# Perceiver block on one core: second values read the stored norm, last residual moved to VectorE, order of the last two batches and of the mean changed

## The reference

```
x = x + xattn(layernorm(x), ctx, mask) @ W_o + b_o   # 8 heads of 64, keys from ctx (8, 2048, 384)
h = layernorm(x)                                     # "the second norm"
x = x + attn(h @ Wq, h @ Wkv) @ Wo                   # 16 heads, attends over the 8 batches' axis
x = x + bitlinear_ffn(layernorm(x))                  # weights rounded to -1, 0, 1 times mean(|w|)
```

## Time and profile before

| what | value |
|---|---|
| runs | 795.01 us median of 3 (793.55 to 796.64) |
| the profiled execution's own time | 799.53 us |
| its span | 797.6 us |
| PE busy | 674.9 us, 85% of the span |
| DVE / ACT / POOL busy | 442.4 / 372.3 / 109.7 us |
| mean granted TensorE clock | 0.931 |

### The profile page before, as it was taken

One profiled execution on the slowest core, in us unless ns is written; L12 is line 12 of the kernel. 1 busy time (PEld: TensorE's weight loads), 2 busy tenths in 40 slices (PEclk: granted clock), 3 DMA queues, 4 the chain that ended last, 5 costly groups with the idle time before them and its releaser, 6 DMA issues.

```text
span 797.6 us, 15089 instructions
## 1 busy us (share of the span) xinstructions
PE 674.9 (85%) x4274; PEld 526.5 (66%) x4274; DVE 442.4 (55%) x972; ACT 372.3 (47%) x872; POOL 109.7 (14%) x152
## 2 busy tenths in 40 slices
PE   3988597969889688969949979999999899889994
PEld 2767486858778577858738757777777778535542
DVE  5742343544535453444547746666666445698860
ACT  3234243424334333434424336666665343478883
POOL 2481000010100110010120002222222100012211
PEclk9998797979989797989969989999999899999998
DMA  8010000000000000003238934444443333001011
GB/s 299 5 44 21 4 19 20 21 21 21 2 20 21 21 2 20 21 21 113 86 119 317 322 112 159 159 159 159 159 159 138 140 122 117 1 1 27 13 27 39
DMA packets 40081, 64.84 MB, mean 81 GB/s; under 512 B 4074, under 2 KB 20458, under 8 KB 40050
## 3 DMA queue, kind: packets, MB, share of 16 engines
q1 hardware_dynamic: 40050, 64.45, 24.2%
HBM read 53.95 MB, written 10.49 MB: 81 GB/s over the span
## 4 chain that ended last, share of the span: by engine, by line
PE 70%; issue 11%; DVE 10%; ACT 3%; DVEq 3%; POOL 1%; DMA 1%; ACTq 0%; SPq 0%; POOLq 0%
PE bank L571 41%; PE bank L706 6%; PE bank L923 5%; PE bank L694 3%; PE bank L931 3%; PE bank L679 2%; PE bank L841 2%; DVE tern L1630 2%; PE bank L818 1%; PE bank L873 1%; DMA wq_raw<-in_L_xattn_W_q_dram 1%; PE bank L829 1%; DVE wqk_odd_lo L1327 1%; ACT cxT_hi L999 1%; DVE h_f L1735 1%
## 5 line engine op out<-in xcount | busy, mean ns | idle before, releaser
L1016 ACT ACTIVATE probs<-probs,negm 128x256 f32<-128x256 f32 x104 | 52.2, 503 | 105.5 <-DVE negm L1452 105.5
L1452 DVE CUSTOM_DVE_ANT_0 probs<-bank,bias,negm_old 128x256 f32<-128x256 f32 x104 | 46.0, 480 | 60.3 <-PE bank L679 58.1
L679 PE MATMUL bank<-kT_hi,qT_hi 64*128 64x256 f32 x104 | 23.2, 443 | 48.6 <-issue 44.5
L923 PE MATMUL bank<-w_T,xqT 128*128 128x512 bf16 x256 | 58.4, 379 | 4.6 <-ACT xqT L1212 2.0
L468 POOL TENSOR_TENSOR rstd<-var_eps,neg_half 128x1 f32 (+1 forms) x16 | 10.4, 652 | 337.8 <-DVE var_eps L1515 265.8
L706 PEld LDWEIGHTS bank<-v_sb,pT 128*128 128x128 f32 x416 | 52.4, 191 | 5.5
L706 PE MATMUL bank<-v_sb,pT 128*128 128x64 f32 x416 | 54.7, 274 | 0.0
L1327 DVE TENSOR_TENSOR kT_lo<-bank,kT_hi 128x512 fp32r<-128x512 f32 x28 | 19.4, 692 | 61.2 <-ACT kT_hi L1005 61.2
L1009 ACT COPY v_sb<-bank 128x512 f32<-128x512 f32 x28 | 15.1, 590 | 76.5 <-PE bank L706 73.5
L679 PEld LDWEIGHTS bank<-kT_hi,qT_hi 64*128 64x128 f32 x104 | 11.4, 214 | 58.3 <-issue 46.7
L923 PEld LDWEIGHTS bank<-w_T,xqT 128*128 128x128 bf16 x256 | 24.1, 98 | 34.8 <-issue 2.9
(11 more groups left out here) (226 smaller groups left out, 1717.1 us busy)
## 6 DMA issues: line engine op xcount, KB each, us to landing
tern_dram<-tern SPq DMA_DIRECT2D x8, 768.0 KB, 5.4
tstage<-tern_dram SPq DMA_DIRECT2D x8, 768.0 KB, 4.7
cx<-in_ctx_dram SPq DMA_DIRECT2D x14, 384.0 KB, 2.9
absw<-in_L_ffn_w_gate_dram SPq DMA_DIRECT2D x8, 512.0 KB, 3.8
absw<-in_L_ffn_w_up_dram SPq DMA_DIRECT2D x8, 512.0 KB, 5.2
absw<-in_L_ffn_w_down_dram SPq DMA_DIRECT2D x8, 512.0 KB, 6.1
tern_raw<-in_L_ffn_w_gate_dram SPq DMA_DIRECT2D x8, 512.0 KB, 6.2
tern_raw<-in_L_ffn_w_up_dram SPq DMA_DIRECT2D x8, 512.0 KB, 7.0
```

The costliest lines, as they stand in the source:

```text
L679: last = mm(bank[3 + j][:, 0:CHUNK], part(qT, a)[o:o + DH, g, :], part(kT, c)[o:o + DH, g, :], start=(a == c), stop=(a == "lo"))
L923: last = mm(bank[3 + 2 * which + c % 2][:], xqT[:, u, k * P:(k + 1) * P], w_T[:, which, k, c * 512:c * 512 + 512], start=(k == 0), stop=(k ...
L1016: fn(probs[:, h, :], probs[:, h, :], ACT.Exp, bias=negm[:, h:h + 1], scale=-1.0, accum_out=csum[:, h:h + 1]).then_inc(p_done, 1)
L1452: nc.vector.tensor_tensor_reduce(probs[:, h, :], bank[3 + h % 2][:, 0:CHUNK], bias[:], -SCALE, negm_old[:, h:h + 1], ALU.add, ALU.min, neg ...
```

## The change

1. The second values read `ln_T` itself instead of the copy `lnT_g`. The copies are gone from ACT, and the loop over groups on PE becomes straight code. The first product waits for each part that it needs and no longer for all of `wv2_lo`.
2. The residual of batch 7 is added by DVE straight from bank 4 (`residual_last`). ACT's copy to `xo` and POOL's addition of that batch are gone.
3. The norms of batches 6 and 7 use two slots of `stats` and `mv` and are interleaved; `values_low` is placed between them in another order.
4. SP issues the first piece of |w| once the last projection has ended, then the store of batch 7, the second piece, and, after all stores have landed, the first query/key weights. Before, all of these waited for the last `norm_low`.
5. DVE runs `weights_low(0)` ahead of the sums of |w| instead of behind them.
6. PE does the mean and the wait for DVE's last value copy between `project(0, 0)` and `project(0, 1)`, instead of ahead of both.

```diff
 # SP
-            with sp.Fori(0, B) as b:
+            def keep_x(b):
                 sp.wait_ge(x_mid, START + b + 1)
-                sp.dma_start(x_mid_dram[bass.ds(b, 1)].rearrange("a p d -> p (a d)"), tile_of(x_all, b)).then_inc(x_mid_out, 16)
-
-            sp.wait_ge(lnT_lo, START + B)
-            sp.wait_ge(x_mid_out, 16 * B)
-            for g in range(G):
-                if g >= 2:
-                    sp.wait_ge(absw_done, START + g - 1)
+                sp.dma_start(x_mid_dram[b], x_all[:, b, :]).then_inc(x_mid_out, 16)
+
+            def load_abs(g):
                 to = absw[g % 2]
...
+            for b in range(B - 1):
+                keep_x(b)
+            sp.wait_ge(xo_ps, START + B)
+            load_abs(0)
+            keep_x(B - 1)
+            load_abs(1)
+            sp.wait_ge(x_mid_out, 16 * B)
+            sp.dma_start(wqk_raw[:, 0:DK, :], wq2_v[:, :, 0:P]).then_inc(wqk_in, 16)
+            sp.dma_start(wqk_raw[:, DK:2 * DK, :], wkv_v[:, :, 0:P]).then_inc(wqk_in, 16)
+            for g in range(2, G):
+                sp.wait_ge(absw_done, START + g - 1)
+                load_abs(g)
 # POOL
-            with pool.Fori(1, B) as b:
+            with pool.Fori(1, B - 1) as b:
                 rsqrt(b - 1, var_c, rstd_c)
                 residual(b)
+            rsqrt(B - 2, var_c, rstd_c)
             rsqrt(B - 1, var_c, rstd_c)
 # PE
-            pe.wait_ge(wv2_lo, START + DK)
-            with pe.Fori(0, G // 2) as t:
...
+            def second_values(g, half):
+                def waits(a, b, k):
+                    if g == 0 and half == 0:
+                        if a == "lo" and k == 0:
+                            pe.wait_ge(lnT_lo, START + B)
+                        elif b == "lo":
+                            pe.wait_ge(wv2_lo, START + k + 1)
+                        elif a == "hi":
+                            pe.wait_ge(wv2_hi, START + k + 1)
+
+                product(bank[2 * (g % 2) + half][:], lambda k, w: part(ln_T, w)[:, k, g * P:(g + 1) * P],
+                        lambda k, w: part(wv2, w)[:, k, half * 512:half * 512 + 512], DK, waits).then_inc(v2_ps, 1)
+
+            pe.wait_ge(lnT_hi, START + B)
+            for g in range(G):
+                if g >= 2:
+                    pe.wait_ge(v2_act, START + g - 1)
+                    pe.wait_ge(v2_dve, START + g - 1)
+                second_values(g, 0)
+                second_values(g, 1)
...
             for u in range(UNITS):
                 project(u, 0)
+                if u == 0:
+                    mean_weights()
+                    pe.wait_ge(v2_dve, START + G)
                 project(u, 1)
 # ACT
             for k in range(DK):
-                if k == DK - 1:
-                    projected(B - 1)
                 cp(wv2.hi[:, k, :], wv2_raw[:, k, :]).then_inc(wv2_hi, 1)
...
-            group_copy(0, 0)
-            group_copy(1, 1)
             weights_high(0)
             with act.Fori(0, G // 2) as t:
...
-                    group_copy(g + 2, u)
 # DVE
+            def residual_last():
+                dve.wait_ge(xo_ps, START + B)
+                dve.wait_ge(x_mid, START + B - 1)
+                tt(x_all[:, B - 1, :], x_all[:, B - 1, :], bank[4][:], ALU.add).then_inc(x_mid, 1)
+
+            norm_stats(B - 2)
             values_low(0)
-            norm_stats(B - 2)
+            residual_last()
+            norm_stats(B - 1, 1)
+            norm(B - 2)
             values_low(1)
-            norm(B - 2)
+            norm(B - 1, 1)
             norm_low(B - 2)
-            norm_stats(B - 1)
             values_low(2)
-            norm(B - 1)
+            norm_low(B - 1)
             values_low(3)
-            norm_low(B - 1)
...
+            weights_low(0)
             with dve.Fori(0, G // 2) as t:
...
-            weights_low(0)
```

More of the change, by code:

```diff
@@ L153, in bass_perceiver_block_kernel @@
         wv2 = Split("wv2", 88, DK, HD2)
-        lnT_g = Split("lnT_g", 48, 2, D)
         absw = [at("absw0", 56, 3, PIECE), at("absw1", 68, 3, PIECE)]
@@ L216, in bass_perceiver_block_kernel @@
         (wq_hi, wk_hi, wo_hi, xnT_hi, q_done, qT_hi, cxT_hi, kT_hi, v_done, p_done, alpha_done, pT_act, onT_hi, lnT_hi, xo_done,
-         wv2_hi, lnTg_done, v2_act, wqk_hi, qT2_done, p2_done, pT2_act, tern_rounded, wo2_hi, oT_hi, wT_act,
+         wv2_hi, v2_act, wqk_hi, qT2_done, p2_done, pT2_act, tern_rounded, wo2_hi, oT_hi, wT_act,
          xq_done, xqT_done, sg_done, h_round, hq_done, hqT_done, y_scaled) = sems(
             "act", "wq_hi wk_hi wo_hi xnT_hi q_done qT_hi cxT_hi kT_hi v_done p_done alpha_done pT_act onT_hi lnT_hi xo_done "
-            "wv2_hi lnTg_done v2_act wqk_hi qT2_done p2_done pT2_act tern_rounded wo2_hi oT_hi wT_act "
+            "wv2_hi v2_act wqk_hi qT2_done p2_done pT2_act tern_rounded wo2_hi oT_hi wT_act "
             "xq_done xqT_done sg_done h_round hq_done hqT_done y_scaled")
@@ L366, in _ @@
                 sp.dma_start(to[:, 2, :].rearrange("p (t i) -> p t i", t=DK), down_v[g]).then_inc(absw_in[g % 2], 16)
-                if g == 0:
-                    sp.dma_start(wqk_raw[:, 0:DK, :], wq2_v[:, :, 0:P]).then_inc(wqk_in, 16)
-                    sp.dma_start(wqk_raw[:, DK:2 * DK, :], wkv_v[:, :, 0:P]).then_inc(wqk_in, 16)
+            for b in range(B - 1):
[10 more added lines that the diff above has]
+                load_abs(g)
             def load_weights(piece, slot):
@@ L778, in _, with mean_weights @@
             turn_norm(B - 1)
-            pe.wait_ge(wv2_lo, START + DK)
-            with pe.Fori(0, G // 2) as t:
[L782 to L791, removed]
+            def second_values(g, half):
[16 more added lines that the diff above has]
+                second_values(g, 1)
+            def mean_weights():
+                pe.wait_ge(asum_done, START + 1)
+                mm(bank[4][:, 0:3], ones[:], asum3[:], start=True, stop=True).then_inc(mean_ps, 1)
             pe.wait_ge(v2_act, START + G)
-            pe.wait_ge(v2_dve, START + G)
             def project(u, which):
@@ L1094, in _ @@
             norm_high(B - 1)
[L1095 to L1103, removed]
             def weights_high(m):
@@ L1507, in norm_low, with norm_stats, norm @@
                 low(of(ln_T.lo), bank[6][:].rearrange("p (k g q) -> p k g q", k=DK, q=16), of(ln_T.hi)).then_inc(lnT_lo, 1)
-            def norm_stats(b):
+            def norm_stats(b, slot=0):
                 dve.wait_ge(x_mid, START + b + 1)
                 settle()
-                own(dve, ln_step_c, 2 * b, nc.vector.bn_stats(stats[:, 0, :], tile_of(x_all, b)), 1)
+                own(dve, ln_step_c, 2 * b, nc.vector.bn_stats(stats[:, slot, :], tile_of(x_all, b)), 1)
                 settle()
-                own(dve, ln_step_c, 2 * b, nc.vector.bn_aggr(mv[:, 0, :], stats[:, 0, :]), 2)
-                ts(var_eps[:, bass.ds(within(b), 1)], mv[:, 0, 1:2], EPS, None, ALU.add).then_inc(var_c, 1)
-            def norm(b):
+                own(dve, ln_step_c, 2 * b, nc.vector.bn_aggr(mv[:, slot, :], stats[:, slot, :]), 2)
+                ts(var_eps[:, bass.ds(within(b), 1)], mv[:, slot, 1:2], EPS, None, ALU.add).then_inc(var_c, 1)
+            def norm(b, slot=0):
                 dve.wait_ge(rstd_c, START + b + 1)
                 dve.wait_ge(lnT_ps, START + b)
-                ts(xn_c[:], tile_of(x_all, b), mv[:, 0, 0:1], rstd[:, bass.ds(within(b), 1)], ALU.subtract, ALU.mult).then_inc(xn_c_done, 1)
+                ts(xn_c[:], tile_of(x_all, b), mv[:, slot, 0:1], rstd[:, bass.ds(within(b), 1)], ALU.subtract, ALU.mult).then_inc(xn_c_done, 1)
             def query_low(b):
@@ L1557, in values_low, with weights_low @@
                 low(wv2.lo[:, k, :], wv2_raw[:, k, :], wv2.hi[:, k, :]).then_inc(wv2_lo, 1)
+            def residual_last():
[3 more added lines that the diff above has]
+            norm_stats(B - 2)
             values_low(0)
-            norm_stats(B - 2)
+            residual_last()
+            norm_stats(B - 1, 1)
+            norm(B - 2)
             values_low(1)
-            norm(B - 2)
+            norm(B - 1, 1)
             norm_low(B - 2)
-            norm_stats(B - 1)
             values_low(2)
-            norm(B - 1)
+            norm_low(B - 1)
             values_low(3)
-            norm_low(B - 1)
+            def weights_low(m):
+                dve.wait_ge(wqk_hi, START + m + 1)
+                low(wqk_lo_of[m % 2][:], wqk_raw[:], wqk_hi_of[m % 2][:]).then_inc(wqk_lo, 1)
+            weights_low(0)
             with dve.Fori(0, G // 2) as t:
@@ L1578, in _ @@
                     tc(v_all[:, bass.ds(g, 1), 512:1024].rearrange("p a n -> p (a n)"), bank[2 * u + 1][:]).then_inc(v2_dve, 1)
-            def weights_low(m):
-                dve.wait_ge(wqk_hi, START + m + 1)
-                low(wqk_lo_of[m % 2][:], wqk_raw[:], wqk_hi_of[m % 2][:]).then_inc(wqk_lo, 1)
-            weights_low(0)
             dve.wait_ge(absw_done, START + G)
```

## The result

The changed kernel is faster. In the comparison that the forecast was made for, it takes 787.9 us (median of 4, 785.57 to 790.62) against 795.83 before (median of 4); the ratio, estimated from all runs of the comparison, is 0.9894, 95% interval 0.9863 to 0.9925, that is 8.4 us (6.0 to 10.9), and the two medians differ by 7.9. Two later comparisons of the same kernels gave 0.9863 (0.9817 to 0.9908) and 0.9848 (0.9812 to 0.9883). The forecast was 784.5 with a range of 781.8 to 789.8. The profiled execution took 788.87 with a span of 786.8; forecast were 789.0 and 787.1.

A forecast was written before the change was run, and what follows sets the result against it. Two chains bound it: the values on PE and the sums of |w| on DVE and DMA. Earlier start 5.8, `project(0, 0)` about 5 and small change made 11.0, taken as 10.5: from 795.0 to 784.5, range 781.8 to 789.8.

The forecast's parts named there:

- The tail: Batches 6 and 7 after the last projection: PE starts the second values at 406.2 instead of 412.00, 5.8 earlier.
- The values: Second values on PE: same matmuls, still 45.27 us without a gap, ending at 451.5; straight code saves nothing.
- the slower rival: PE waits for its own straight code: one extra instruction fetch gives no change (794), two give 804; chance 0.03.
- The new wait: DVE's first sum and ACT's first value copy now wait behind query/key weights; first sum 414.6, no PE stall.
- W: Landing time of the first query/key weights, which sets the chain of sums; forecast 412.4.
- The rival of late weights: Query/key weights land at 416.7, PE stalls at group 2, sums move; gain 6.5, time 788.5; chance 0.16.
- The sums: Sums of |w| on DVE: first at 414.6, eighth at 451.1, mean at 455.3 instead of 461.6.
- The product in the wait: `project(0, 0)` on PE moved into the wait for the mean, clock kept high: about 5 us of the gain.
- S: Time from the start of the last projection's last block to unit 0's scores on PE; forecast 62.4, before 73.4.
- The clock: Rival: PE's clock falls waiting for the mean; at 2.5 or more, 12 matmuls cost some 2 us more; chance 0.10.
- signs that I had named as making me wrong: A gap at group 2, a clock of 0.50 after the mean, or a shift that shrinks in later units.
- The sum: Total at unit 0's key copy: ends at 459.5 instead of 470.5, a gain of 11.0, taken as 10.5.

## Why the prediction was right

**The tail.** Forecast start of the values 9.0 after the last block, measured 8.3 to 8.5. The step that I had too dear was `rstd` of batch 7: I let it end behind `values_low(1)`, and it ended 0.5 after that had begun. What `xn_c` of batch 7 (402.84) then waited for was DVE itself, busy with `values_low(1)`. Undoing the interleaved order and the residual out of PSUM together costs 4.2 of start, and undoing the direct read of `ln_T` 1.9; that is 6.1 of the 6.3 by which the start moved (14.8 to 8.5). How the 4.2 divide between order and residual no run shows.

**The values.** 45.9 on PE (405.89 to 451.78), and 46.5 in each of the other two profiles, against the 45.3 of the earlier trace rows. There was no gap; the clock stood at 0.50 longer at their start (about 4 us in the first profile and 6 in the second, against 3 before), which I hadn't allowed for. The page counts 18 instruction fetches where there were 17; no gap of PE shows in the values, so the slower rival found no ground.

**The new wait.** The landing of the weights, W, was the number on which most hung: 15.2 forecast, 15.1, 14.9 and 14.9 measured. The store took 6.5 from issue to landing behind piece 0, neither the 2.0 nor the 8.8 of the earlier trace rows. The transfers came in by their order of issue: the last part of piece 0 at 406.0 (399.67 + 6.3), the store at 406.7, the last part of piece 1 at 411.2 (402.01 + 9.2), the weights at 412.7. The issues in the changed kernel's trace, KB and us to landing:

```profile
absw<-in_L_ffn_w_down_dram SPq DMA_DIRECT2D x1, 512.0 KB, 6.3
x_mid_dram<-x_all SPq DMA_DIRECT2D x1, 256.0 KB, 6.5
...
absw<-in_L_ffn_w_down_dram SPq DMA_DIRECT2D x1, 512.0 KB, 9.2
```

The Trainium skill, "DMA: Bandwidth & Descriptors", section "Queues, rings and completion order", says that each DMA engine takes a queue's descriptors in ring order and that a semaphore's increment lands only after that engine's earlier writes. This trace agrees. The landing of piece 1, 13.6 after the block, was forecast at 13.9. PE had no wait at group 2 in the changed kernel, and 2.6 when W came 2.8 later (SP's order of before). That shows both the mechanism and that there was almost nothing to spare. The rival of late weights is priced by 4.3 of W, which from the 10.5 taken leaves 6.2 and not 6.5; its condition did not occur. One thing I had overlooked: SP issues the weights only when all eight stores have landed, though by the kernel's addresses `wqk_raw` (4 KB per partition from 8 KB on) lies on batches 4 and 5 of `x_all` alone. So the 6.5 of the last store stands in the chain ahead of W without need of the memory. No run issued the weights ahead of that landing, and what it would bring is open.

**The sums.** The first sum was right to 0.3. The stretch from the second to the eighth was the term that I mis-sized: 32.2 in the trace of before and 32.6 in the forecast, but 33.4, 32.5 and 35.3 in the three profiles (for the first, 452.23 minus 418.79). I took one sample for a constant. With the first sums 0.1 to 0.3 early, it moved the mean by +0.6, -0.4 and +2.2 from the forecast 58.1. The sums waited for their loads in all three, the eighth by 2.5, 1.8 and 2.3.

**The product in the wait.** With `project(0, 0)` ahead of the mean, PE's wait for it shrank from 4.3 (457.3 to 461.6) to 1.7, to about none, and to 2.5 in the three profiles. Taking that back costs 5.4 to 8.2 of S, and doing it alone brings 0.0, both by S. With the product moved, the subtraction may as well stand behind sums that start early: undoing the fifth part showed no loss.

**The clock.** In the first profile the rival came true, and with it one of the signs that I had named as making me wrong, a clock of 0.50 after the mean, although the wait was under 2.5. The windows of that kernel around the mean at 456.33:

```profile
455.00:456.00 1.00, 0.00 (x0) 0.00 (x0) 1.00 (x2) 0.34 (x1) 0.00 (x0) 1.00 0.07 26
456.00:457.00 1.00, 0.67 (x4) 0.63 (x5) 0.49 (x4) 0.00 (x0) 0.00 (x0) 1.00 0.05 16
457.00:458.00 1.00, 1.00 (x6) 0.83 (x5) 0.93 (x3) 0.00 (x0) 0.00 (x0) 0.94 0.81 242
458.00:459.00 1.00, 1.00 (x3) 0.74 (x3) 1.00 (x3) 0.79 (x1) 0.00 (x0) 0.50 1.05 399
```

The 12 matmuls of `project(0, 1)` took 4.2 where those of the kernel with `weights_low(0)` behind the second sum took 3.0. That is 1.2 of the 1.8 by which S of this profile exceeds the forecast 62.4; the other 0.6 is the later mean. In the third profile PE waited 2.5 and the clock stayed at 1.00. My bound of 2.5 for the fall was not one.

**The sum.** S shrank by 9.3, 11.7 and 9.0 where 11.0 was worked out and 10.5 taken; the ratios give 8.4, 10.9 and 12.1 us. The mean came 5.7, 6.7 and 4.0 earlier, and the part from it to the scores went from 9.1 to 5.5, 4.0 and 4.1. The prediction books 5.8 of the gain as the earlier start of the values. That start is needed, but it did not set the time by itself: in the first and the third profile the mean waited for the sums, and the start alone would have been held up by them. The forecast was 3.4 below the first median, of which the baseline of that comparison, 795.83 instead of 795.01, is 0.8. That the profiled span came out at 786.8 for a forecast of 787.1 is luck: it shrank by 10.8, of which 9.3 is S, less 0.4 for a later start of the last block, and 1.9 fell behind the scores. Of that 1.9, the first product of `project_out` is 1.4 (8.5 before, 7.1 after), by when the clock rose; the change doesn't touch it, and the other two profiles of the changed kernel gave 7.3 and 5.7.

## What to carry to other kernels

When two chains end almost together, price a change by both, and measure every part also alone: here the move of the mean gave nothing by itself and over 5 us of S with its partners. A transfer that is needed first should be judged by what stands ahead of it in its queue. And a duration that is made of loads is a range, not a number: take several of its samples before resting a tenth of the result on it.

## What the runs showed that I had not expected

- The clock fell after PE had been back at work for over 1 us following a wait of 1.7, and did not fall after waits of 2.1 (`weights_low(0)` behind the sums) and 2.5 (the changed kernel's third profile). The length of a wait alone did not decide it.
- The first product of `project_out`, 24 matmuls and the same code in all these kernels, took anything from 5.7 to 8.5 us, by the clock at its start, and the first stage of one and the same kernel differed by 4.0 us (393.6 to 397.6). Marks counted from a common event inside the trace told variants apart that the total times could not, though each rests on one execution.
